# Two normalisations from one set of statistics at the seam between two attention layers

## What is computed

```python
h = tokens(x)                              # FFT magnitudes by rings, projected
h = layernorm(h + attention0(h))           # no gain, no bias: (x - m) / sqrt(v + eps)
# the next block, its input called x:
    n = layernorm(x) * g + b               # normalises once more, what was just normalised
    x = x + attention1(n)
    t = layernorm(x) * g2 + b2
    out = x + mixture_of_experts(t)        # 8 experts, the best 2 per token
h = layernorm(x + out)
```

## Time and profile before

| What | Value |
|---|---|
| median of three runs | 886.38 us |
| the profiled execution's own time | 886.28 us |
| its span, first to last instruction | 884.4 us |
| busy share PE / DVE / ACT / POOL | 86% / 60% / 49% / 51% |
| granted TensorE clock, mean | 0.924 of full speed |
| the last output projection of `att0` on PE | ends at 634.06 us |
| the first transpose of `att1` on PE | starts at 641.67 us |
| the last instruction of DVE in `att0` | ends at 645.18 us |

### The profile page before, as it was taken

The page is one execution under the profiler, slowest core; times in us unless marked ns, Lnnn a source line. Parts: engine busy times, 40 slices in busy tenths (PEclk is TensorE's granted clock), DMA queues, the critical chain, the costliest instruction groups (busy, mean ns, idle before and its releaser), DMA issues. The chain is left out here.

```text
span 884.4 us, 16768 instructions
## 1 busy us (share of the span) xinstructions
PE 759.8 (86%) x5845; PEld 648.5 (73%) x5846; DVE 527.6 (60%) x988; ACT 432.7 (49%) x840; POOL 454.8 (51%) x371
## 2 busy tenths in 40 slices
PE   5999999999999702598787977999899998999996
PEld 5888888888888501498786866967557775899995
DVE  4899999999999603254434542769848764222213
ACT  1777777777777801234333532524133321555561
POOL 4578777778777506676576656300242033444420
PEclk9999999999999955789898978999999987999997
DMA  9744548855688276444444445220000473111103
GB/s 235 220 123 131 140 117 245 221 151 143 175 239 250 121 209 174 132 139 129 120 140 116 116 117 142 73 74 2 2 1 2 188 213 108 50 53 52 46 26 115
DMA packets 72986, 111.71 MB, mean 126 GB/s; under 512 B 8391, under 2 KB 52396, under 8 KB 72556
## 3 DMA queue, kind: packets, MB, share of 16 engines
q1 hardware_dynamic: 60014, 75.66, 30.1%
q0 software_dynamic: 11776, 34.62, 13.8%
q10 hardware_dynamic: 1152, 0.84, 0.3%
HBM read 91.04 MB, written 20.06 MB: 126 GB/s over the span
## 5 line engine op out<-in xcount | busy, mean ns | idle before, releaser
L551 PE MATMUL psum<-power,tT 128*128 128x192 f32 x864 | 169.9, 355 | 81.4 <-DVE tT L663 61.7
L551 PEld LDWEIGHTS psum<-power,tT 128*128 128x128 f32 x864 | 157.5, 209 | 91.4 <-issue 70.6
L492 POOL DMA_INDIRECT rows<-power_table,rank_row x144 | 147.6, 1025 | 102.0 <-issue 41.6
L295 PE MATMUL ps<-dft,fold 112*112 112x97 f32 x1536 | 170.2, 265 | 18.5 <-POOL fold L262 10.3
L295 PEld LDWEIGHTS ps<-dft,fold 112*112 112x112 f32 x1536 | 164.5, 180 | 27.2 <-DVE folded L367 15.3
L269 POOL TENSOR_TENSOR ss<-uv 97x388 f32<-97x388 f32 x96 | 119.4, 1266 | 77.9 <-ACT uv L335 77.9
L663 DVE SCALAR_TENSOR_TENSOR tT<-rows,swaps,scaled 128x384 f32<-128x384 f32 x144 | 81.3, 613 | 93.0 <-remote 45.8
L367 DVE TENSOR_TENSOR folded<-ps,far 112x388 f32<-112x388 f32 x192 | 98.6, 554 | 18.2 <-ACT far L323 18.2
L262 POOL TENSOR_TENSOR fold<-img 112x896 f32<-112x896 f32 x48 | 101.9, 2123 | 12.4 <-DMA img<-in_x 6.8
L602 ACT ACTIVATE scaled<-rows,swaps 128x384 f32<-128x384 f32 x144 | 77.7, 604 | 60.5 <-DMA rows<-power_table,rank_row 44.9
L384 DVE TENSOR_TENSOR uv<-ps,odd 97x388 f32<-97x388 f32 x192 | 98.6, 555 | 14.3 <-ACT odd L328 12.7
(11 more groups left out here) (177 smaller groups left out, 956.1 us busy)
## 6 DMA issues: line engine op xcount, KB each, us to landing
img<-in_x SPq DMA_DIRECT2D x48, 784.0 KB, 5.1
power_table<-power SPq DMA_DIRECT2D x16, 576.0 KB
power<-in_w_tok SPq DMA_DIRECT2D x3, 1728.0 KB, 10.4
power_table<-power SPq DMA_DIRECT2D x1, 4656.0 KB
power<-in_w SPq DMA_DIRECT2D x8, 579.0 KB, 7.8
power<-in_w SPq DMA_DIRECT2D x4, 1152.0 KB, 10.7
rows<-power_table,rank_row POOLq DMA_INDIRECT x144
expert_inputs<-normed SPq DMA_DIRECT2D x3, 288.0 KB, 2.3
```

Source lines behind the costliest of these rows:

```text
L295: last = pe.matmul(ps1[0:HALF, j % 2, i, col:col + FREQ], fold[:, j // UPG % FOLD_RING, part, x0:x0 + HALF], dft[:, part * FREQ:(part + 1) ...
L492: pool.indirect_dma_start(out=rows[:, j % RING, half, :], out_offset=None, in_=table[0:RECORDS if j < PLAIN else ROWS, :], in_offset=bass. ...
L551: last = pe.matmul(ps[:, q % 2, 0:DIM], points[:, j % SWAPPED, c, s].rearrange("p h b -> p (h b)"), wt[:, c, s, chunk, :], start=(chunk == ...
```

## The change

There are three parts. First, DVE takes one set of statistics per chunk in `att0`. POOL computes from the same variance a second root, `both_roots` = (v * (1 + eps) + eps^2)^-0.5, ahead of the plain one. DVE writes `normed` straight from z, with the mean and `both_roots` (`twice_normalised`). Second, the plain normalisation of `x_all` moves behind all three chunks of that. Third, PE no longer waits for `normed` = 3 between the layers, but for `z_done` = 9 (the last addition of `att0`, whose PSUM places the transposes use); ACT and POOL have no wait there any more, DVE keeps its own; and six of the seven filler matmuls go.

```diff
+        "both_roots": sb("both_roots", [P, TT, 1]),
-        "st_next": ..., "mv_next": ...
...
 program_pool:
-        for c in range(NC if L1 else NC + 1):
-            if c < NC:
-                pool.wait_ge(stat1, 2 * (c + 1))
-                inverse_root(pool, W, mv[:, c * 3:c * 3 + 3, 1:2], pow1, 2 * c)
-            if not L1 and c >= 1:
-                pool.wait_ge(stat0, 2 * c)
-                inverse_root(pool, W, B["mv_next"][:, c * 3 - 3:c * 3, 1:2], pow0, 2 * (c - 1))
+        for c in range(NC):
+            pool.wait_ge(stat1, 2 * (c + 1))
+            var = mv[:, c * 3:c * 3 + 3, 1:2]
+            if not L1:
+                root = both_roots[:, c * 3:c * 3 + 3, :]
+                pool.tensor_scalar(root, var, 1.0 + EPS, EPS * EPS, ALU.mult, ALU.add).then_inc(pow0, 1)
+                pool.wait_ge(pow0, 2 * c + 1)
+                pool.tensor_tensor(root, root, W["minus_half"]..., ALU.pow).then_inc(pow0, 1)
+            inverse_root(pool, W, var, pow1, 2 * c)
...
 program_tensor:
-            busy_work(pe, W, psum[:, V_BANK, :], 7)
+            busy_work(pe, W, psum[:, V_BANK, :], 1)
...
 program_vector:
+        def twice_normalised(c):
+            dve.wait_ge(pow0, 2 * (c + 1))
+            for t in range(c * 3, c * 3 + 3):
+                last = dve.tensor_scalar(W["normed"][:, t, :], z[:, t, :], mv[:, t, 0:1], both_roots[:, t, :], ALU.subtract, ALU.mult)
+            last.then_inc(xin_done, 1)
...
-            if 1 <= c <= NC:
-                normalise(dve, c - 1, z, mv, W["normed"] if L1 else x_all, pow1, normed)
-                if not L1:
-                    dve.wait_ge(normed, c)
-                    statistics(dve, c - 1, x_all, B["st_next"], B["mv_next"], stat0)
-            if not L1 and c >= 2:
-                normalise(dve, c - 2, x_all, B["mv_next"], W["normed"], pow0, xin_done)
+            if c >= 1:
+                if L1:
+                    normalise(dve, c - 1, z, mv, W["normed"], pow1, normed)
+                else:
+                    twice_normalised(c - 1)
+        if not L1:
+            for c in range(NC):
+                normalise(dve, c, z, mv, x_all, pow1, normed)
...
+    def added(eng):
+        eng.wait_ge(z_done, TT)
...
 between the layers:
-            att0[-1](pool)
-            att0[-1](pe)
+            att0[-2](pe)
-            att0[-1](act)
```

More of the change, by code:

```diff
@@ L729, in attention_buffers @@
         "mv": sb("mv", [P, TT, 2]),
-        "st_next": sb("st_next", [P, TT, 6]),
-        "mv_next": sb("mv_next", [P, TT, 2]),
+        "both_roots": sb("both_roots", [P, TT, 1]),
     }
@@ L787, in attention @@
     t_tr, tT_done, twice = [S(n) if L1 else None for n in ("t_tr", "tT", "twice")]
-    stat0, pow0 = [S(n) if not L1 else None for n in ("stat0", "pow0")]
+    pow0 = S("pow0") if not L1 else None
+    both_roots = B["both_roots"]
     xin_done = W["xin_done"]
@@ L879, in program_pool @@
                     spread_k(pool, c, h, k_plain[:, h, first * SEQ:last_img * SEQ]).then_inc(k_spread, 1)
-        for c in range(NC if L1 else NC + 1):
-            if c < NC:
-                pool.wait_ge(stat1, 2 * (c + 1))
-                inverse_root(pool, W, mv[:, c * 3:c * 3 + 3, 1:2], pow1, 2 * c)
-            if not L1 and c >= 1:
-                pool.wait_ge(stat0, 2 * c)
-                inverse_root(pool, W, B["mv_next"][:, c * 3 - 3:c * 3, 1:2], pow0, 2 * (c - 1))
+        for c in range(NC):
[5 more added lines that the diff above has]
+                pool.wait_ge(pow0, 2 * c + 1)
+                pool.tensor_tensor(root, root, W["minus_half"][:, :, None].to_broadcast([P, 3, 1]), ALU.pow).then_inc(pow0, 1)
+            inverse_root(pool, W, var, pow1, 2 * c)
             if L1:
@@ L1163, in program_vector @@
         by_units([(1, mask_and_max), (2, sums), (1, place_v), (3, share_out)])
-        for c in range(NC + 1 if L1 else NC + 2):
+        def twice_normalised(c):
[3 more added lines that the diff above has]
+            last.then_inc(xin_done, 1)
+        for c in range(NC + 1):
             if c < NC:
@@ L1190, in done @@
             eng.wait_ge(twice, NC)
-    return program_sync, program_pool, program_tensor, program_scalar, program_vector, done
+    return program_sync, program_pool, program_tensor, program_scalar, program_vector, added, done
 def experts(nc, ctx, sem, W, x_all, xs, results, out, attention_done):
```

## The result

The changed kernel takes 878.00 us (median of 20 runs, 873.02 to 883.49); the kernel before takes 885.57 (median of 20 runs, 877.69 to 888.97). The ratio is 0.993, its 95% interval 0.9912 to 0.9948: 4.6 to 7.8 us less. 880.0 was forecast, in a range from 871 to 884.5, and 6.3 us less than before.

What follows compares the result with a forecast made beforehand. At the seam between the attentions DVE's chain was taken to bound the kernel, PE waiting for `x_all`. Projections 6.36 us earlier less a 0.1 us stall gave 6.3: 886.28 - 6.3 = 880.0 us, range 871 to 884.5.

Steps and rivals of the forecast that it cites:

- step 3: Seam, PE: first transposes of the second attention start at 635.33 us, 6.34 us earlier than before.
- (4): Seam, DVE chunk 1: second joint normalisation ends at 637.37, so PE's second transposes start at 637.42, 6.36 us earlier.
- (5): Seam, PE: first projections start at 638.98, 6.36 us earlier; ACT's copy of chunk 0 is not late.
- (6): Seam, DVE chunk 2: waits some 0.9 us for its joint root, runs from 638.25; plain chunks end at 641.7.
- (7): Chunk 0's keys on DVE: start 641.8, end 646.7, the next late point; PE stalls 0 to 0.3 us, taken 0.1.
- Steps 1 to 7: The seam between the attentions: positions of DVE, PE and POOL pieces, from chunk 0's joint normalisation to its keys.
- Step 8: Waits between the layers: those taken from ACT and POOL give nothing; removed statistics and moved normalisations are already counted by position.
- The rule against the trace: POOL beside DVE's normalisations: rows showed up to 0.14 us delay, the Trainium skill exclusion for a whole instruction; sum followed rows.
- DVE becomes the bound at the keys: Rival: normalisations delay joint roots 0.93 us each, PE stalls 1.8 us, 881.8 us; with slower normalisations only, 880.7; chance 0.11.
- PE loses its clock: Rival at the seam: with six fillers gone the clock falls for one stretch, giving back 5 us: 885; chance 0.06.
- Slower than before: Rival: low clock through all the seam's projections, 15.2 us more less 6.3, 8.9 us slower: 895.2; chance 0.03.
- The other level of this kernel's runs: Rival: runs mostly at a lower level, as one at 877.69, perhaps from clock stretches around 736 us: 871.4; chance 0.20.

Runs made afterwards that it cites:

- e7: Changed kernel plus three unread normalisation-like instructions on VectorE between the last plain chunk and the keys; 0.70 us lost in chunk 1's projections, one profile.
- e6: Changed kernel with ScalarE and GpSimd waiting for normed = 3 between the layers as before; ratio 1.0009 to the kernel before.
- e2: Changed kernel with seven fillers and PE waiting for normed = 3 again, keeping the new statistics and order; ratio 1.0011 to the kernel before.
- e10: Changed kernel run again unaltered; median 878.50 us, ratio 0.994 to the kernel before.
- e4: Changed kernel without its three fillers at the seam, behind the last projection and around the second transposes; ratio 0.9912 to the kernel before.
- e8: Changed kernel with joint roots of chunks 0 and 1 first, VectorE reordered, the filler ahead of the projections removed; ratio 0.9914 to the kernel before.
- e9: Kernel before with one filler in the place of seven behind the last output projection; 15.69 us at the seam, 2.14 more than before.
- e5: Changed kernel with each plain chunk normalised directly behind its joint one, not all three at the end; ratio 0.9933 to the kernel before.
- e3: Kernel before with only the waits changed: PE for z_done = 9, ScalarE and GpSimd for nothing; ratio 0.9991 to the kernel before.

## Why the prediction was right, and where it was not

| Step of the prediction | forecast | measured (+ 0.76) |
|---|---|---|
| first transposes (step 3) | 635.33 | 635.35 |
| second transposes (4) | 637.42 | 637.46 |
| first projections (5) | 638.98 | 639.02 |
| third `twice_normalised` (6) | 638.25 | 638.15 |
| keys of chunk 0 start (7) | 641.8 | 641.82 |
| PE's stall at the keys (7) | 0 to 0.3, taken 0.1 | none |
| gain at chunk 1's projections (sum) | 6.3 | 6.32 |

**Steps 1 to 7** held, each to 0.1 us, because every piece of the new order had a row of the same shape in the trace before, and the waits could be laid out from start to start. e7 shows that the point named as late next is the right one. The moment of that point was taken a little too early: "a quarter of 9.91 / 2" is 1.24 us, but the chunk's first matmuls are its widest (16 of 391 columns, then 16 of 323) and start 0.33 us apart, so the fifth, the first of the second half of the keys, starts 1.34 us behind the first. So there was a little more room than forecast, and the stall of 0.1 us that was booked did not come.

**Step 8 failed in its first half.** "The waits taken from ACT and POOL give nothing" was argued from the kernel before, where ACT's copy would have waited for the transposes in any case. With the transposes moved ahead of `x_all`, ACT's old wait is the later of the two, and e6 lost 7.85 us with it in place, 5.36 of them to the wait itself and the rest where the clock fell. The sum was right since the change does remove the wait, but its worth was booked at zero. The cost of a wait has to be read at the new positions, not the old ones.

**The rule against the trace, and "DVE becomes the bound at the keys".** POOL's powers in the changed kernel took 0.86 to 0.96 us. Of those that ran mostly or wholly beside normalisations one took 0.88 (from 632.64) and one 0.93 (from 637.76), and one that ran half beside them 0.96:

```profile
635.14 0.96 POOL L736 TENSOR_TENSOR mv<-mv,minus_half 128x3 f32<-128x3 f32 x1
...
636.49 0.87 POOL L887 TENSOR_TENSOR both_roots<-both_roots,minus_half 128x3 f32<-128x3 f32 x1
```

None was held up for 0.93 us; the third joint root ended at 637.36, 0.1 us ahead of the forecast, and the keys were not late. The longest power beside normalisations in any profile took 1.08 us (e2 and e10), 0.2 over its usual time. The prediction priced this rival too high: its 0.93 us is a row of three normalisations, and one instruction is about 0.31. Its smaller case also has a slip, since 0.5 us off the gain gives 880.5 and not 880.7. The exclusion for a whole instruction that the Trainium skill states (SBUF — State Buffer, "Who interferes with whom") is for VectorE in a two-port mode. No instruction here was held up for a whole one of the other engine. But no row shows that these normalisations ran in such a mode: they follow each other every 0.28 to 0.30 us, hardly faster than the additions that read PSUM (0.30 to 0.31). So the sum stood, and the rule was not put to the test.

**The rivals.** "PE loses its clock" did not happen in the changed kernel (1.00 from 626 to 660 us), but e4 shows that its mechanism is near: without the three fillers that stayed at the seam the clock did fall. Of these the third can go (e8); the first two were not tried apart. The six that went were not needed any more. "Slower than before" needed over 12 us of it; in e4, e6 and e9 the clock was back by 640, 650 and 650 us, before the projections of chunk 0 were over.

**"The other level of this kernel's runs" was wrong as a case.** There are no two levels: 20 runs of before fill 877.69 to 888.97 us and 20 of after 873.02 to 883.49. I looked for its cause in the clock around the router. The profiles put most of it in the rings' stage, 226.6 to 236.9 us in 13 profiles whose code there is the same. What makes that stage longer (the gathers' landing, or PE's clock in it) I did not take apart. The stage that I had named has a smaller part in it: from the last output projection of `att1` to the end the same 13 profiles took 171.6 to 176.1 us, at a mean clock of 0.91 in the longest and 0.93 in the shortest. These are e5 and e10, columns as in the earlier trace rows:

```profile
707.47:883.59 176.12, 162.97 (x1135) 143.03 (x1134) 54.09 (x167) 72.74 (x226) 58.19 (x57) 0.91 0.27 80
701.17:872.81 171.64, 159.47 (x1135) 140.33 (x1134) 54.11 (x167) 72.83 (x226) 58.16 (x57) 0.93 0.28 82
```

That the median moved by 7.6 us and the seam by 6.3 needs no further cause: 6.3 lies within the interval of 4.6 to 7.8. That interval also answers the prediction's remark that a difference of 1% is about what can be told from none: with 20 runs of each kernel, 0.7% was told from none.

## What to carry to other kernels

Where an engine waits for several things at once, lay all engines out at the new positions before a part is called worthless: here the shorter work gave nothing without PE's new wait (e2), the new waits nothing without the shorter work (e3), ACT's old wait alone took the whole gain back (e6), and all together gave 6.3 us. A filler that holds the clock belongs to the wait that it fills; when the wait shrinks, it turns from a gain of 2.1 us into a cost of 4.5. For a change of under 1% a distance between two instructions in the profile shows the parts (7.23 and 7.22 us in two profiles), where the times of the same kernel spread over 10 us and twenty of each show the sum only.

## What the runs showed of the hardware that was not expected

- In e4 PE did two groups of six transposes, with 1.27 and 1.25 us of idle time ahead of them and no filler, and the granted clock fell to 0.50 (1.2 GHz) ahead of the second group (1.00 up to 636 us, 0.56 on average from 636 to 637); it read 1.00 again from 640 us on. With one filler ahead of the transposes and one between them (e8), or a third behind them (changed kernel), it stayed at 1.00 (2.4 GHz).
- In e9, where PE did nothing for 6.74 us, the clock was 0.50 from 640 us and 0.81 on average from 648 to 650: it stayed low through transposes and two fillers, and was back for the projections.
- The same stage with indirect gathers lasts from 226.6 to 236.9 us from one execution to the next, and the stretch from the last output projection of `att1` to the end from 171.6 to 176.1, where the mean granted clock is 0.93 in the shortest and 0.91 in the longest.
